# The first two tiles of a four-layer residual chain interleaved: the second tile's narrow chunk moved ahead of the first tile's later chunks

## The chip, the core and the metric

One core of a Trainium2 chip runs the whole program. The metric is the device time of one execution in microseconds (us). TensorE (PE) multiplies matrices, VectorE (DVE), ScalarE (ACT) and GpSimd (POOL) work on elements, SyncE (SP) issues most of the transfers. PEld is PE's loading of stationary operands, beside its matmuls. Each engine works through its own list in order, and semaphores tie the lists together.

## The reference

`x` has 64 batches of 32 rows of 512. Four layers follow each other, each added to its input. The start of the program, which the change touches, is all in the first of them:

```python
def lora_add(base, inp, A, B):
    Ab = A[layer_idx][lora_indices]
    Bb = B[layer_idx][lora_indices]
    t = jnp.einsum('bri,bni->bnr', Ab, inp)
    return base + jnp.einsum('bor,bnr->bno', Bb, t) * SCALE
gate = lora_add(jnp.einsum('bnh,fh->bnf', x, W_gate), x, A_gate, B_gate)
up = lora_add(jnp.einsum('bnh,fh->bnf', x, W_up), x, A_up, B_up)
act = jax.nn.silu(gate) * up
down = lora_add(jnp.einsum('bnf,hf->bnh', act, W_down), act, A_down, B_down)
...
x = x + _L0_cond_ref(...)
x = x + _L1_cond_ref(x, itok_B_0_15, L1_cond_weights)
x = x + _L2_cond_ref(...)
x = x + _L3_cond_ref(x, L3_cond_weights, itok_B_0_15)
```

F is 1376, the rank is 16, and each batch picks its own adapter (A and B) by an index. Layers 1 and 3 multiply each batch by a small matrix of its own, layer 2 is a projection with a routed adapter.

## The kernel before

The 2048 rows are cut into 16 tiles of 128 rows (four batches each). The first layer runs over all tiles, then the other three do. F is cut into three chunks: chunk 0 is the narrow one with 352 columns, chunks 1 and 2 have 512. A step is one chunk of one tile; before the change step s is chunk `s % 3` of tile `s // 3`. I write (tile, chunk), so (1,0) is the narrow chunk of the second tile.

Every float32 operand of a matmul is split in two parts, a high one that ACT writes (a cast, `hi`) and a low one that DVE writes (raw minus high, `lo`); for the weights `wd` of the down product POOL writes the low part instead. `product` is then three matmuls (lines 1050 to 1052), `stacked` two (1057 and 1058). The weights are loaded and split once, in the beginning, and stay.

For one tile PE does: `gate` and `up` of a chunk (12 matmuls each, over four pieces of 128 of the 512 inputs); `x_a`, x times the chosen adapters A, which from the second tile on is part of the narrow chunk's gate matmuls (480 columns instead of 352 and 128); `transpose_t`, after DVE has masked that result (`tm`, line 846); `adapters` (four matmuls, the B part, which ends the chunk); `transpose_act`, after ACT's silu (`gate` job, line 691) and DVE's product with up (line 885); `down` (18 matmuls for chunk 0, 24 for the others, adding up in `down_ps`); and once for a tile `transpose_td` and `down_adapters`, after DVE's mask `td`. The gate and up of a step stand in one of two pairs of PSUM banks.

The adapters come by indirect transfers that POOL issues: `a` (four gathers for a tile, one for each batch) and `b` (one for each chunk), `bd` one for each tile. `a_raw` holds one tile, so the next tile's gathers wait until both of its splits are done: `at`, for `x_a`, and `adt`, for the down side. `b_sel` has two slots: the gather of step s waits until the adapters of step s - 2 have run.

The order of the splits and of the silus is written by hand in `lane_jobs(s)`, one list for ACT and DVE both, and `gathers(s)` with the `wd` pieces of that list gives POOL's order. `plain_loads(s)` orders SP's loads.

Of the kernel before, what the change touches and what calls it, by code (L numbers as in the profile page):

```python
# [68 lines left out]
W13_FIRST = 6  # L69
# [58 lines left out]

def plain_loads(s):

    i, n = divmod(s, NC)
    if s < 0:
        first = wgu_items(0, 0)
        return ([("x", 0, 0), first[0], first[1], ("x", 0, 1)] + first[2:] + wgu_items(0, 1)
                + wgu_items(1, 0) + [("wd", f) for f in pieces_of(0)] + wgu_items(1, 1)
                + wgu_items(2, 0) + [("wd", f) for f in pieces_of(1)] + wgu_items(2, 1)
                + [("x", 1, 0)] + [("wd", f) for f in pieces_of(2)])
    return [("x", i + 1, 0)] if n == 0 and 1 <= i < NT - 1 else []


def gathers(s):
# [59 lines left out]
NO_SPLIT = ("gate", "tm", "x1")  # L201


def bass_conditioned_residual_chain(nc, x_t, x_rows, it_lora, it_cond, it_lang, wgu, wd, a_all, b_d,
# [7 lines left out]
    with ExitStack() as ctx:  # L212
# [1118 lines left out]
```

## Time and profile before

| | us |
|---|---|
| median of three runs (610.81 to 610.93) | 610.91 |
| the profiled execution | 610.14 |
| its span | 608.3 |
| PE busy in the span | 574.6 |
| DVE, ACT, POOL busy | 324.8, 204.8, 232.2 |

The profiled execution is 0.77 us shorter than the median, and its time is its span and 1.84 us around it. PE is busy in 94% of the span. The span's slices of a fortieth are 15.2 us each: the first 60 us, nearly four of them, hold 20.5 of the 33.7 us in which PE isn't busy (39.54 us of them are busy).

### The profile page before, as it was taken

How to read it: one execution, taken by the hardware profiler on the slowest of the kernel's cores; microseconds unless marked ns; L12 is line 12 of the kernel's file. 1: busy time of each engine (PE TensorE's matmuls, PEld its weight loads, DVE VectorE, ACT ScalarE, POOL GpSimd, SP SyncE). 2: the span in 40 equal slices, each digit the busy share in tenths (PEclk: the TensorE clock that was granted, in tenths of full speed). 3: DMA queues.
4: the chain of work that ended last, by engine and by line, in shares of the span. 5: the costliest groups of instructions: out<-in, count | busy, mean ns of one | idle time of the engine just before them, and what ended most of it. 6: DMA issues, size and time to landing. Idle time of an engine off the chain costs nothing.

```text
span 608.3 us, 8713 instructions
## 1 busy us (share of the span) xinstructions
PE 574.6 (94%) x3359; PEld 515.5 (85%) x3359; DVE 324.8 (53%) x686; ACT 204.8 (34%) x413; POOL 232.2 (38%) x238
## 2 busy tenths in 40 slices
PE   4578999999999999999999999999999998999896
PEld 3467898989898988898988989898989888988894
DVE  3596434344344444343534344434444668899986
ACT  3654233233233232332323332332332433343331
POOL 4276425243443434332313131323322435556631
PEclk9689999999999999999999999999999999999999
DMA  8951524242434242433333242423334310322211
GB/s 271 367 180 52 170 75 135 75 136 80 130 110 122 99 141 88 129 101 114 109 94 130 75 131 73 132 73 130 97 108 152 126 53 19 99 76 70 71 70 70
DMA packets 30281, 68.99 MB, mean 113 GB/s; under 512 B 4704, under 2 KB 9120, under 8 KB 30240
## 3 DMA queue, kind: packets, MB, share of 16 engines
q0 software_dynamic: 10752, 37.23, 19.5%
q1 hardware_dynamic: 19344, 31.17, 15.5%
q8 instruction: 27, 0.44, 0.3%
q14 instruction: 14, 0.11, 0.1%
q10 hardware_dynamic: 144, 0.03, 0.0%
HBM read 60.03 MB, written 8.39 MB: 112 GB/s over the span
## 4 chain that ended last, share of the span: by engine, by line
PE 80%; DVE 11%; DMA 2%; issue 2%; ACT 2%; POOL 1%; SPq 1%; POOLq 0%; DVEq 0%; ACTq 0%
PE gu_ps L1050 13%; PE gu_ps L1052 13%; PE gu_ps L1051 13%; PE down_ps L1050 7%; PE down_ps L1051 7%; PE down_ps L1052 7%; PE gu_ps L1057 3%; PE gu_ps L1058 3%; PE act_t L1116 3%; PE l_ps L1050 2%; PE l_ps L1052 2%; PE l_ps L1051 2%; DVE route L949 2%; DVE x L967 2%; DVE route L948 1%
## 5 line engine op out<-in xcount | busy, mean ns | idle before, releaser
L576 POOL DMA_INDIRECT b_sel_raw<-b_gu,idx_rank x48 | 45.7, 952 | 225.4 <-PE gu_ps L1058 222.3
L1050 PE MATMUL gu_ps<-w_sb,xt 128*128 128x512 f32 x256 | 105.8, 413 | 4.4 <-DVE w_sb L837 4.4
L1050 PE MATMUL down_ps<-wd_sb,act_hl 128*128 128x288 f32 (+1 forms) x352 | 105.1, 298 | 0.2 <-DVE act_hl L837 0.2
L1051 PE MATMUL down_ps<-wd_sb,act_hl 128*128 128x288 f32 (+1 forms) x352 | 103.8, 295 | 0.0
L1052 PE MATMUL down_ps<-wd_sb,act_hl 128*128 128x288 f32 (+1 forms) x352 | 103.7, 295 | 0.0
L1052 PE MATMUL gu_ps<-w_sb,xt 128*128 128x512 f32 x256 | 101.8, 397 | 0.0
L1051 PE MATMUL gu_ps<-w_sb,xt 128*128 128x512 f32 x256 | 101.4, 396 | 0.0
L576 POOL DMA_INDIRECT a_raw<-a_all,idx_batch x64 | 76.1, 1190 | 48.1 <-DVE wd_sb L837 28.7
L698 ACT CAST act_hl<-act_t 128x256 fp32r<-128x256 f32 (+1 forms) x64 | 27.3, 452 | 149.6 <-PE act_t L1116 149.6
L691 ACT ACTIVATE act<-gu_ps 128x512 f32<-128x512 f32 (+1 forms) x48 | 26.5, 553 | 132.7 <-PE gu_ps L1058 132.6
L837 DVE TENSOR_TENSOR act_hl<-act_t,act_hl 128x256 fp32r<-128x256 f32 (+1 forms) x64 | 32.0, 520 | 70.3 <-ACT act_hl L698 70.3
L885 DVE TENSOR_TENSOR act<-act,gu_ps 128x512 f32<-128x512 f32 (+1 forms) x48 | 30.3, 632 | 73.1 <-ACT act L691 73.1
L1050 PEld LDWEIGHTS down_ps<-wd_sb,act_hl 128*128 128x128 f32 (+1 forms) x352 | 66.1, 188 | 1.7 <-DVE act_hl L837 0.4
L1051 PEld LDWEIGHTS down_ps<-wd_sb,act_hl 128*128 128x128 f32 (+1 forms) x352 | 66.2, 188 | 1.2
L1052 PEld LDWEIGHTS down_ps<-wd_sb,act_hl 128*128 128x128 f32 (+1 forms) x352 | 66.1, 188 | 0.0
L837 DVE TENSOR_TENSOR b_sel<-b_sel_raw,b_sel 128x1024 fp32r<-128x1024 f32 (+1 forms) x48 | 53.8, 1121 | 15.3 <-ACT b_sel L675 15.3
L1050 PEld LDWEIGHTS gu_ps<-w_sb,xt 128*128 128x128 f32 x256 | 48.8, 191 | 13.4 <-issue 3.1
L1052 PEld LDWEIGHTS gu_ps<-w_sb,xt 128*128 128x128 f32 x256 | 48.8, 190 | 11.1
L1051 PEld LDWEIGHTS gu_ps<-w_sb,xt 128*128 128x128 f32 x256 | 49.1, 192 | 7.2
L675 ACT CAST b_sel<-b_sel_raw 128x1024 fp32r<-128x1024 f32 (+1 forms) x48 | 45.6, 950 | 3.3 <-DMA b_sel_raw<-b_gu,idx_rank 3.3
L1050 PE MATMUL l_ps<-w2ra_hl,x2t_hl 128*128 128x328 f32 (+1 forms) x128 | 42.8, 334 | 1.3 <-DVE x_res L876 1.0
L1051 PE MATMUL l_ps<-w2ra_hl,x2t_hl 128*128 128x328 f32 (+1 forms) x128 | 39.8, 311 | 0.0
(126 smaller groups left out, 1121.4 us busy)
## 6 DMA issues: line engine op xcount, KB each, us to landing
w_sb_raw<-wgu SPq DMA_DIRECT2D x16, 256.0 KB, 8.1
x_res<-x_rows SPq DMA_DIRECT2D x16, 256.0 KB, 3.3
x_after_l<-x_res SPq DMA_DIRECT2D x16, 256.0 KB, 2.1
x<-x_after_l SPq DMA_DIRECT2D x16, 256.0 KB, 2.7
xt_raw<-x_t SPq DMA_DIRECT2D x15, 256.0 KB, 2.5
out<-y SPq DMA_DIRECT2D x15, 256.0 KB, 2.0
wd_sb_raw<-wd SPq DMA_DIRECT2D x10, 256.0 KB, 8.7
w2ra_hl_raw<-w2ra_t SPq DMA_DIRECT2D x4, 324.0 KB, 4.8
```

The source lines that it names most:

```text
L576: nc.gpsimd.indirect_dma_start(out=dst, out_offset=None, in_=table, in_offset=bass.IndirectOffsetOnAxis(ap=idx, axis=0)).then_inc(s, 16)
L675: sc.copy(out_, in_).then_inc(s_hi, 1)
L691: sc.activation(act[:, s % 2, 0:width(s % NC)], gate_of(s), ACT.Silu).then_inc(s_silu, 1)
L698: ins = sc.copy(act_hl[0:k, s % 2, 0, j0:j1, :], act_t[0:k, j0:j1, :])
L837: return ve.tensor_tensor(out_, raw, high.bitcast(F32), ALU.subtract)
L885: ve.tensor_tensor(a, a, up_of(s), ALU.mult).then_inc(s_mul, 1)
L1050: pe.matmul(out_, stationary[0], moving[0], start=start, stop=False, skip_group_check=True)
L1051: pe.matmul(out_, stationary[0], moving[1], start=False, stop=False, skip_group_check=True)
L1052: return pe.matmul(out_, stationary[1], moving[0], start=False, stop=stop, skip_group_check=True)
L1057: pe.matmul(out_, stationary, moving[0], start=False, stop=False, skip_group_check=True)
L1058: return pe.matmul(out_, stationary, moving[1], start=False, stop=True, skip_group_check=True)
L1116: mm = pe.transpose(act_t[0:w, j, :], act[:, s % 2, j * P:j * P + w], ident)
```

## The change

The first six steps get another order, `ORDER`: (0,0), (0,1), (1,0), (0,2), (1,1), (1,2). From the third tile on the steps are as before. What PE does from the start to the adapters of (2,0) is written out call by call, and there (0,0) is followed at once by gate and up of (1,0), ahead of `x_a(0)`. Steps are numbered by their place in `ORDER`, so `gate(2)` is the gate of (1,0) and `adapters(4)` those of (1,1); `down(d)` and `transpose_act(d)` count as before, tile by tile, so `down(2)` is that of (0,2). Gate and up of (1,0) stand in the banks of `down_ps`, which are not in use yet, and its act in the second half of `x_res`. For the second tile `x_a` is a call of its own too. `t_hl` gets two slots.

The lists of ACT, DVE, POOL and SP for these steps are written out as well. The load and the split of the second tile's x go up ahead of everything of chunks 1 and 2, the computation of the indices for the `b` gathers goes up on DVE into the split of the first weights, and POOL has a list of its own, `pool_jobs`. The indices of the later layers are computed two steps later (`s == 4`), and their gathers start two steps later (`W13_FIRST`).

```diff
-W13_FIRST = 6
+W13_FIRST = 8
...
+ORDER = [(0, 0), (0, 1), (1, 0), (0, 2), (1, 1), (1, 2)] + [(i, n) for i in range(2, NT) for n in range(NC)]
+FREE = 6
...
+def slot(s):
+    return (0, 1, 2, 0, 1, 0)[s] if s < FREE else (s + 1) % 2
...
+def first_items():
+    w = wgu_items(0, 0)
+    return [("x", 0, 0), w[0], w[1], ("x", 0, 1), w[2], w[3]] + wgu_items(0, 1) + [("x", 1, 0)]
...
 def plain_loads(s):
-    i, n = divmod(s, NC)
     if s < 0:
-        first = wgu_items(0, 0)
-        return ([("x", 0, 0), first[0], first[1], ("x", 0, 1)] + first[2:] + wgu_items(0, 1)
-                + wgu_items(1, 0) + [("wd", f) for f in pieces_of(0)] + wgu_items(1, 1)
-                + wgu_items(2, 0) + [("wd", f) for f in pieces_of(1)] + wgu_items(2, 1)
-                + [("x", 1, 0)] + [("wd", f) for f in pieces_of(2)])
-    return [("x", i + 1, 0)] if n == 0 and 1 <= i < NT - 1 else []
-
-
-def gathers(s):
-
-    i, n = divmod(s, NC)
-    if s < 0:
-        return [("a", 0, b) for b in range(TB)] + [("b", 0), ("b", 1)]
+        return (first_items() + wgu_items(1, 0) + wgu_items(1, 1) + wgu_items(2, 0) + wd_items(0) + wgu_items(2, 1)
+                + wd_items(1) + wd_items(2))
+    if s == 4:
+        return [("x", 2, 0)]
+    i, n = ORDER[s]
+    return [("x", i + 1, 0)] if n == 0 and 2 <= i < NT - 1 else []
...
+def pool_jobs(s):
+    if s < FREE:
+        return {-1: a_items(0) + [("b", 0), ("b", 1)],
+                0: a_items(1) + [("b", 2)],
+                1: [("b", 3)] + wd_items(0) + [("bd", 0)],
+                2: wd_items(1) + [("b", 4)] + a_items(2),
+                3: [("b", 5)] + wd_items(2),
+                4: [("b", 6)],
+                5: [("bd", 1)]}[s]
...
+    if s <= FREE:
+        w2u = wgu_items(2, 1)
+        return {-1: first_items() + [("at", 0)],
+                0: wgu_items(1, 0) + [("tm", 0), ("b", 0), ("t", 0), ("adt", 0)] + wgu_items(1, 1)
+                + [("b", 1), ("gate", 0)],
+                1: wgu_items(2, 0) + wd_items(0) + [("gate", 1), ("at", 1), ("act", 0), w2u[0], w2u[1], ("tm", 1),
+                                                    w2u[2], w2u[3]],
+                2: [("b", 2), ("t", 1), ("b", 3), ("gate", 2), ("adt", 1)],
+                3: [("gate", 3)] + wd_items(1) + [("act", 1), ("b", 4)],
+                4: [("gate", 4), ("bd", 0), ("act", 2)] + wd_items(2) + [("b", 5), ("x", 2, 0)],
+                5: [("tdm", 0), ("td", 0), ("act", 3), ("x1", 0), ("at", 2), ("gate", 5), ("b", 6)],
+                6: [("act", 4), ("tm", 2), ("act", 5), ("t", 2), ("adt", 2), ("bd", 1), ("tdm", 1), ("gate", 6),
+                    ("b", 7)]}[s]
-    if s < 0:
-        first = wgu_items(0, 0)
-        return [("x", 0, 0), first[0], first[1], ("x", 0, 1)] + first[2:] + wgu_items(0, 1) + [("at", 0), ("b", 0)]
-    if s == 0:
-        return ([("tm", 0), ("t", 0)] + wgu_items(1, 0) + [("gate", 0)] + [("wd", f) for f in pieces_of(0)]
-                + [("adt", 0)] + wgu_items(1, 1) + [("b", 1)])
-    if s == 1:
-        return ([("act", 0)] + wgu_items(2, 0) + [("wd", f) for f in pieces_of(1)] + [("gate", 1)] + wgu_items(2, 1)
-                + [("b", 2)])
-    if s == 2:
-        return ([("act", 1), ("x", 1, 0), ("at", 1), ("gate", 2)] + [("wd", f) for f in pieces_of(2)]
-                + [("b", 3), ("adt", 1)])
...
+        t_hl = sb("t_hl", [2, 2, P], F32R, mem_a)
...
+        def bank(s, m):
+            return gu_ps[slot(s)][m][:] if slot(s) < 2 else down_ps[:, m, :]
...
+        def act_of(s):
+            w = width(ORDER[s][1])
+            return act[:, slot(s), 0:w] if slot(s) < 2 else x_res[:, 1, 0:w]
...
+                for job in pool_jobs(s):
...
-                    if job == ("at", 0):
+                    if job == ("wgu", 0, 0, 2):
...
-                if s == 2:
+                if s == 4:
...
-            for s in range(STEPS):
-                i, n = divmod(s, NC)
+            def whole(part, s):
+                part(s, 0, HC)
+
+            whole(gate, 0)
+            whole(up, 0)
+            whole(gate, 2)
+            whole(up, 2)
+            x_a(0)
+            gate(1, 0, HC // 2)
+            transpose_t(0)
+            gate(1, HC // 2, HC)
+            adapters(0)
+            whole(up, 1)
+            adapters(1)
+            whole(gate, 3)
+            x_a(1)
+            transpose_act(0)
+            up(3, 0, HC // 2)
+            transpose_t(1)
+            up(3, HC // 2, HC)
+            adapters(2)
+            adapters(3)
+            down(0)
+            whole(gate, 4)
+            transpose_act(1)
+            whole(up, 4)
+            adapters(4)
+            down(1)
+            transpose_act(2)
+            gate(5, 0, HC // 2)
+            down(2)
+            gate(5, HC // 2, HC)
+            transpose_td(0)
+            transpose_act(3)
+            up(5, 0, HC // 2)
+            down_adapters(0)
+            up(5, HC // 2, HC)
+            adapters(5)
+            down(3)
+            transpose_act(4)
+            whole(gate, 6)
+            down(4)
+            transpose_act(5)
+            whole(up, 6)
+            transpose_t(2)
+            down(5)
+            adapters(6)
+            for s in range(FREE + 1, STEPS):
```

On POOL, the stretch from the second tile's `a` gathers on. `a_raw` are the `a` gathers, `b_sel_raw` the `b` gathers (`b_gu1` is chunk 1's table), TENSOR_TENSOR the low parts of `wd`. Before:

```order
L576 DMA a_raw<-a_all,idx_batch 128x304 x2
L576 DMA b_sel_raw<-b_gu2,idx_rank 128x1024
L645 TENSOR_TENSOR wd_sb<-wd_sb_raw,wd_sb 128x2x256 x4
L576 DMA a_raw<-a_all,idx_batch 128x304 x2
L576 DMA b_sel_raw<-b_gu0,idx_rank 128x704
L645 TENSOR_TENSOR wd_sb<-wd_sb_raw,wd_sb 128x2x256 x4
L576 DMA bd_hl_raw<-b_d,idx_rank 128x512
L576 DMA b_sel_raw<-b_gu1,idx_rank 128x1024
```

And with the change, from the same gathers on:

```order
L642 DMA a_raw<-a_all,idx_batch 128x304 x4
L642 DMA b_sel_raw<-b_gu0,idx_rank 128x704
L642 DMA b_sel_raw<-b_gu2,idx_rank 128x1024
L708 ISA
L708 TENSOR_TENSOR wd_sb<-wd_sb_raw,wd_sb 128x2x256 x2
L708 TENSOR_TENSOR wd_sb<-wd_sb_raw,wd_sb 96x2x256
L642 DMA bd_hl_raw<-b_d,idx_rank 128x512
L708 TENSOR_TENSOR wd_sb<-wd_sb_raw,wd_sb 128x2x256 x4
L642 DMA b_sel_raw<-b_gu1,idx_rank 128x1024
L642 DMA a_raw<-a_all,idx_batch 128x304 x4
```

All low parts of `wd` now come after the second tile's `a` gathers, and the second table-1 gather, which is that of (1,1), stands right behind the four low parts of chunk 1's `wd`.

On ACT, the place of the `wd` casts (each line here is the high part of what its name says, ACTIVATE is the silu). Before:

```order
L675 CAST w2_sb<-w2_sb_raw 128x512 x4
L675 CAST wd_sb<-wd_sb_raw 128x2x256 x4
L691 ACTIVATE act<-gu_ps1_0 128x512
L675 CAST w2_sb<-w2_sb_raw 128x512 x4
L675 CAST b_sel<-b_sel_raw 128x1024
L698 CAST act_hl<-act_t 128x512
```

And with the change:

```order
L738 CAST b_sel<-b_sel_raw 128x1024
L754 ACTIVATE x_res<-down_ps 128x352
L742 CAST wd_sb<-a_raw 128x11x32 x2
L754 ACTIVATE act<-gu_ps0_0 128x512
L738 CAST wd_sb<-wd_sb_raw 128x2x256 x4
L761 CAST act_hl<-act_t 128x512
L738 CAST b_sel<-b_sel_raw 128x1024
L754 ACTIVATE act<-gu_ps1_0 128x512
L738 CAST bd_hl<-bd_hl_raw 128x512
L761 CAST act_hl<-act_t 128x512
L738 CAST wd_sb<-wd_sb_raw 128x2x256 x4
```

The casts of chunk 1's `wd` stood ahead of the silu of (0,1); now they stand behind the silu of (0,2), and those of chunk 2 behind the high part of (0,2)'s transposed act.

On DVE, what stands around the second tile's `at` (the low part `wg0_sb<-a_raw`, which `x_a(1)` needs). Before:

```order
L837 TENSOR_TENSOR act_hl<-act_t,act_hl 128x512
L837 TENSOR_TENSOR xt1<-xt1_raw,xt1 128x512
L837 TENSOR_TENSOR wg0_sb<-a_raw,wg0_sb 128x4x128
L885 TENSOR_TENSOR act<-act,gu_ps0_1 128x512
L837 TENSOR_TENSOR b_sel<-b_sel_raw,b_sel 128x704
```

And with the change:

```order
L900 TENSOR_TENSOR w2_sb<-w2_sb_raw,w2_sb 128x512 x4
L948 TENSOR_TENSOR act<-act,gu_ps1_1 128x512
L900 TENSOR_TENSOR wg0_sb<-a_raw,wg0_sb 128x4x128
L900 TENSOR_TENSOR act_hl<-act_t,act_hl 128x256
L900 TENSOR_TENSOR act_hl<-act_t,act_hl 96x128
L900 TENSOR_TENSOR w2_sb<-w2_sb_raw,w2_sb 128x512 x2
```

It moved from behind all weights of gate and up to ahead of the last four of them, chunk 2's up weights.

## Rows read from the trace of the kernel before

**Rows 1.** The profile's page: PE's share; the clock granted in 40 equal slices.
```profile
PE 574.6 (94%) x3359; PEld 515.5 (85%) x3359; DVE 324.8 (53%) x686; ACT 204.8 (34%) x413; POOL 232.2 (38%) x238
PEclk9689999999999999999999999999999999999999
```

**Rows 2.** PE's waits, first 130 us: what for, us in total, times, longest.
```profile
PE gu_ps L1050 <- DVE wg_sb L837: 10.9, 2, 6.5
PE gu_ps L1050 <- DVE w_sb L837: 4.4, 2, 2.9
PE t_ps L1096 <- DVE t_m L846: 4.0, 2, 2.6
PE gu_ps L1057 <- DVE t_hl L837: 1.0, 1, 1.0
```

**Rows 3.** PE's timeline: start, duration, operation, [idle before and releaser].
```profile
17.14 0.33 PE L1050 MATMUL gu_ps<-wg_sb,xt 128*128 128x128 f32 x1 [4.37 <-DVE wg_sb L837]
...
17.75 0.27 PE L1052 MATMUL gu_ps<-wg_sb,xt 128*128 128x128 f32 x1
...
40.60 0.47 PE L1050 MATMUL gu_ps<-w_sb,xt 128*128 128x512 f32 x1 [2.91 <-DVE w_sb L837]
...
42.12 0.63 PE L1050 MATMUL gu_ps<-w_sb,xt 128*128 128x512 f32 x1
...
44.68 0.94 PE L1116 MATMUL act_t<-const_sb,act 128*128 128x128 f32 x4
45.38 0.48 PE L1050 MATMUL gu_ps<-w_sb,xt 128*128 128x512 f32 x1
...
49.10 0.29 PE L1050 MATMUL down_ps<-wd_sb,act_hl 128*128 128x288 f32 x1
...
52.26 0.38 PE L1050 MATMUL gu_ps<-wg_sb,xt 128*128 128x480 f32 x1
...
55.21 0.41 PE L1050 MATMUL gu_ps<-wu_sb,xt 128*128 128x352 f32 x1
...
92.13 0.40 PE L1050 MATMUL gu_ps<-w_sb,xt 128*128 128x512 f32 x1
```

**Rows 4.** ACT's timeline, four places.
```profile
15.68 0.62 ACT L679 CAST wg_sb<-a_raw 128x512 fp32r<-128x512 f32 x1 [5.05 <-DMA a_raw<-a_all,idx_batch]
...
49.30 0.60 ACT L691 ACTIVATE act<-gu_ps 128x512 f32<-128x512 f32 x1 [2.02 <-PE gu_ps L1058]
49.80 2.17 ACT L675 CAST wd_sb<-wd_sb_raw 128x512 fp32r<-128x512 f32 x4
...
63.82 1.04 ACT L675 CAST b_sel<-b_sel_raw 128x1024 fp32r<-128x1024 f32 x1
```

**Rows 5.** DVE's timeline, four places.
```profile
23.39 2.50 DVE L837 TENSOR_TENSOR w_sb<-w_sb_raw,w_sb 128x512 fp32r<-128x512 f32 x4
...
27.81 1.16 DVE L837 TENSOR_TENSOR wd_sb<-a_raw,wd_sb 128x352 fp32r<-128x352 f32 x1 [1.37 <-ACT wd_sb L679]
...
34.54 5.92 DVE L837 TENSOR_TENSOR w_sb<-w_sb_raw,w_sb 128x512 fp32r<-128x512 f32 x1
...
64.89 1.23 DVE L837 TENSOR_TENSOR b_sel<-b_sel_raw,b_sel 128x1024 fp32r<-128x1024 f32 x1 [0.41 <-ACT b_sel L675]
```

**Rows 6.** POOL's timeline, three places.
```profile
9.37 0.95 POOL L576 DMA_INDIRECT a_raw<-a_all,idx_batch  x1 [0.30 <-issue]
...
27.30 1.28 POOL L645 TENSOR_TENSOR wd_sb<-wd_sb_raw,wd_sb 128x512 fp32r<-128x512 f32 x1
...
34.91 4.99 POOL L645 TENSOR_TENSOR wd_sb<-wd_sb_raw,wd_sb 128x512 fp32r<-128x512 f32 x4
```

**Rows 7.** Gathers, issue to landing: `a` at 5 to 10 us, at 30.5 to 33 us, `b` at 40 to 100 us.
```profile
DMA to landing us min/median/max: 5.5/6.2/6.8
...
DMA to landing us min/median/max: 3.6/3.9/4.2
...
DMA to landing us min/median/max: 3.4/3.9/4.5
```

More of the change, by code:

```diff
@@ L118, with step_of, slot_before, down_no @@
 CONSTS = const_array()
+ORDER = [(0, 0), (0, 1), (1, 0), (0, 2), (1, 1), (1, 2)] + [(i, n) for i in range(2, NT) for n in range(NC)]
+FREE = 6
+def step_of(i, n):
+    return ORDER.index((i, n))
+def slot(s):
+    return (0, 1, 2, 0, 1, 0)[s] if s < FREE else (s + 1) % 2
+def slot_before(s):
+    return max((k for k in range(s) if slot(k) == slot(s)), default=None)
+def down_no(s):
+    i, n = ORDER[s]
+    return i * NC + n
+def gu_done(i):
+    return step_of(i, NC - 1) + 1
 def x_pieces(i):
@@ L272, in bass_conditioned_residual_chain @@
         banks_a = ExitStack()
-        gu_ps = [[ps(f"gu_ps{i}_{m}", [H], banks_a) for m in range(2)] for i in range(2)]
+        gu_ps = {i: [ps(f"gu_ps{i}_{m}", [H], banks_a) for m in range(2)] for i in (1, 0)}
         down_ps = ps("down_ps", [2, H], banks_a)
@@ L637, in _ @@
             for s in range(-1, STEPS):
-                first = [it for it in gathers(s) if s < 0 or it[0] == "b"]
-                for it in first:
-                    gather_item(it)
-                for job in lane_jobs(s):
+                for job in pool_jobs(s):
                     if job[0] == "wd":
@@ L645, in _ @@
                         pool.tensor_tensor(l, raw, h.bitcast(F32), ALU.subtract).then_inc(s_wdlo, 1)
-                for it in gathers(s)[len(first):]:
-                    gather_item(it)
+                    else:
+                        gather_item(job)
                 if s == STEPS - 2:
@@ L879, in job_lo @@
                     s = job[1]
-                    i, n = divmod(s, NC)
-                    if n == 0 and i >= 1:
-                        mask_td(i - 1)
                     ve.wait_ge(s_silu, s + 1)
-                    a = act[:, s % 2, 0:width(n)]
+                    a = act_of(s)
                     ve.tensor_tensor(a, a, up_of(s), ALU.mult).then_inc(s_mul, 1)
@@ L895, in job_lo @@
                 elif kind == "t":
-                    ins = lo(t_hl[TR:, :, :], t_ps[TR:, 0:2, :], t_hl[TR:, :, :])
+                    own = t_hl[TR:, job[1] % 2, :, :]
+                    ins = lo(own, t_ps[TR:, 0:2, :], own)
                 elif kind == "td":
@@ L1130, in down @@
                         pe.wait_ge(s_wdlo, WD_ORDER.index(f) + 1)
-                    a_hl = [act_hl[0:w, s % 2, part, j, :] for part in range(2)]
+                    a_hl = [act_hl[0:w, d % 2, part, j, :] for part in range(2)]
                     for half in range(2):
@@ L1232, in _ @@
                 if n == 0:
-                    if i == 0:
-                        x_a(0)
                     transpose_t(i)
@@ L1239, in _ @@
                     transpose_x2(0)
-                if s >= 1:
-                    down(s - 1)
+                down(s - 1)
                 if n == 0:
```

142 lines of the change are left out of this document (81 added, 61 removed).

## The prediction, as put on record before the changed kernel had run

> **What bounds the kernel now.** The page comes first: PE is busy in 94% of the span, and the clock row falls below 9 in two slices only, the second (6) and the third (8) [rows 1]. So the kernel is bound by PE's own work, and what is left to gain in the beginning is holes and slow clock. The waits of PE name the holes: 10.9 us for `wg_sb` (6.5 of them the first load, the rest the 4.37 us ahead of `x_a(0)`), 4.4 us for weights, 4.0 for the mask of t and 1.0 for its low part [rows 2]. The timeline of PE then gives the price of each piece of work at the full clock: from 45.38 to 49.10 us there are 16 matmuls of 512 columns, 0.2325 us each, so a gate or up of 512 columns takes 2.79 us and its adapters 0.93; by columns a gate of 352 takes 1.92 and its adapters 0.64. Down takes 3.16 us for four pieces (49.10 to 52.26) and 2.37 for three. From 52.26 to 55.21 stand a gate of 480 columns (2.62) and the transposes of act, which leaves 0.33 for these. `x_a` takes 12 times 0.61 / 5, 1.46 us [rows 3].
>
> With these prices all of PE's work up to the first matmul of (2,1), at 92.13 us, comes to 63.4 us: four blocks of 352 columns (7.7) and eight of 512 (22.3) for the two tiles, adapters 5.0, downs 17.4, transposes and the down adapters 3.6, one `x_a` 1.5, the 128 extra columns of the second tile's gate 0.7, and 5.2 for (2,0). PE starts at 6.5 [rows 2], so 22.2 us are lost by then: 13.8 in the holes of [rows 2], the other 8.4 to half clock and restarts. After 92.13 nothing in the program changes its order in a way that I expect to matter: the later gathers and indices are moved by two steps where PE doesn't wait, and `t_hl` gets a second slot where nobody waited for one. So I forecast the time of that one matmul, and the difference is that of the kernel.
>
> **The change, part by part.** *Gate and up of (1,0) ahead of `x_a(0)`.* PE ended up(0,0) at 12.8 us and idled 4.37 [rows 3]. The three small index operations now ahead of the third weight's split cost it about 0.25. Then 2 x 1.92 us of new work lie in the hole, to 16.8. `x_a(0)` still starts at 17.14, since the gathers of `a` land at 15.68 as before and their cast and low part take 1.46 to the first matmul [rows 3, 4]. All but 0.3 us of the hole is filled.
>
> *Up to the gate of (0,2).* DVE needs 2.50 us for four weights [rows 5], from 17.1 to 19.6, then the mask of t, so the transposes of t come at 20.1 (a hole of 0.2) and adapters(0) end at 22.45. `adt(0)` stands ahead of chunk 1's up weights and ends at 22.75; the first of these is ready at 23.4, a hole of 0.9. Up(0,1) ends at 26.2, adapters(1) at 27.25, gate(0,2) at 30.2. PE has then done 19.4 us of work in 23.7, and 3.8 of that is (1,0)'s.
>
> *`x_a(1)`.* Its gathers wait for `adt(0)`. With 0.95 + 0.30 us each [rows 6] the last of the four is issued at 26.8. At 30 us, under as full a DMA, such gathers landed 3.6 to 4.2 us after issue, and at 5 to 10 us 5.5 to 6.8 [rows 7]; the later stretch is the nearer one, since SP's backlog is the same, and 3.9 gives 30.7, and 1.46 more 32.2. PE, done with gate(0,2) at 30.2, idles. DVE's low part, at 31.4, meets POOL: its two `b` gathers end at 30.3 and then come three low parts of `wd`, about 1.25 us each. The rows show two outcomes of such a meeting. At 27.81 DVE came into a running POOL operation (27.30 to 28.58) and ended 0.4 after it. At 34.54 it took 5.92 us for 0.65 us of work, until POOL had done all four, at 39.90 [rows 5, 6]. I take the first, 32.4 us; the second gives 34.6. The Trainium skill's page "SBUF — State Buffer", section "Who interferes with whom", says that a DVE operation with two SBUF inputs and a GpSimd operation that reads SBUF exclude each other, the later one waiting for the whole of the earlier. By that rule the wait would be to the end of one operation, as at 27.81; the row at 34.54 is worse than the rule.
>
> *From there to the end of adapters(3), which I call T.* `x_a(1)` and the transposes of act end at 34.2. The cast, the low part and the first of chunk 2's up weights (0.55 + 0.63 + 0.63, from rows 4 and 5, and the hand-overs) let up(0,2) start at 36.2, a second hole of 2.0. DVE then has in a row four weights (2.5), a mask (0.5), the low parts of b(1,0), t and b(0,2) (0.9, 0.4, 1.15), from 35.5 to 40.9; adapters(3) follow. T is 42.0. By then PE has done 25.9 us of a total that is now 64.1 (`x_a(1)` apart costs 0.7 more), and 38.2 are left. Without a further hole the mark would stand at 80.2, 11.9 ahead of 92.13.
>
> *adapters(4), of (1,1).* This is where I expect the lead to go. The `b` gather of (1,1) stands on POOL behind the four low parts of chunk 1's `wd`, their casts on ACT behind the silu of (0,2), and this behind adapters(3). After T: silu 0.2 later and 0.5 long before the next [rows 3, 4], first cast 0.7, so POOL starts at T + 1.4; 4.99 for four [rows 6]; gather issued at T + 6.5; landing 3.9 (3.4 to 4.5) [rows 7]; cast and low part of b 2.3 (63.82 to 66.12) [rows 4, 5]. That is T + 12.8. PE has down(0), gate and up of (1,1) and transposes until then, 2.37 + 2.79 + 0.33 + 2.79 = 8.3. The hole is 4.5 us, 4.0 to 5.1 by the bounds of the landing.
>
> *The clock.* After the 4.37 us hole and after the 2.91 us hole the granted clock fell to 1.2 GHz: from 42.12 to 44.68 six matmuls took 0.427 each, and it was back by 45.38 [rows 3]. A hole of 4.5 us should do the same. Each microsecond at the low clock loses 0.46; with 3.3 us of it 1.5 are lost, and the second slice's 6 shows that it can last longer [rows 1]. I take 2.0, with 0 and 2.7 as bounds. The two holes around `x_a(1)`, 2.2 and 2.0 with 1.8 of work between, are each shorter than 2.91, and I take no clock loss there.
>
> *down(2), of (0,2).* Its `wd` casts stand behind the cast of its own act. From the start of its transposes, POOL starts 1.8 later, and a piece is ready every 1.25, where PE needs one each 0.79. PE would end 4.9 after the transposes began and ends 7.6 after; the low parts of b(1,2) and of the third tile's x on DVE meet the same POOL operations and cost one more, 1.1, and the mask of td behind them some 0.3. I take 4.1, with 2.7 and 5.0 as bounds.
>
> The sum: 42.0 + 38.2 + 4.5 + 2.0 + 4.1, and 0.3 for restarts, is 91.1, against 92.13: 1.0 us less. The profiled execution took 610.14, so 609.1 there, and 609.9 against the median, which is 0.77 above that execution.
>
> **The rivals.** *The later holes are cheaper* (0.22). The clock stays up after the hole and b lands in 3.4 instead of 3.9: 2.0 + 0.5 less, 607.4. For it speaks that at 40.60 PE resumed at the full clock and only by 42.12 had lost it, so that a fall isn't certain [rows 3]; against it, that both holes of this length were followed by one.
>
> *POOL holds DVE off at `x_a(1)`* (0.24), the one that ends slower. DVE waits for all three low parts of `wd`: `x_a(1)` at 34.6 instead of 32.4. The hole is then 4.4 us, as long as the one ahead of 17.14, and the half clock falls on up(0,2), another 1.6: 613.7. It decides for slower from a start of `x_a(1)` at about 34.5, or 33.5 with the clock down. For it speaks the row at 34.54; gathers that land in 6.2 us would end in the same place.
>
> *The change does what its order seems made for* (0.06): the gathers and `wd` parts are ready in time, and the lead of 11.9 stays: 599. The chain behind T is four POOL operations and a gather in one queue, so I see little for it.
>
> **How the numbers follow.** The forecast's own case has 0.46, with 608.4 to 611.4 as its range. About 0.2%, 1.2 us, is what a measurement of this kernel can tell from no change. Of the 0.46, 0.15 lie over 1.2 us faster, 0.26 within and 0.05 slower; the cheaper holes, the full gain and 0.01 of the rest are faster, POOL's hold and 0.01 of the rest slower. That makes 0.44, 0.26 and 0.30. The range of 606.3 to 614.0 leaves out the full gain, the bottom of the cheaper case and the top of the slower one.
>
> **What would show it.** Right: PE has no hole over 1 us between 6.54 and 30; one of about 2 ahead of `x_a(1)`; one over 4 ahead of adapters(4), ended by the low part of b, whose gather follows four low parts of `wd` on POOL; matmuls of down(2) in groups of six every 1.25 us with POOL as what they wait for; the first matmul of (2,1) at 91. Wrong: a `b` gather of (1,1) that lands before PE has done up(1,1); a hole at the transposes of t or at up(0,1) much above 1 us, because ACT has more to cast early than I counted; or a change after the 92 us mark.

## The result, and the profile after

The changed kernel takes 615.56 us (median of 4 runs, 614.74 to 616.72), the kernel before 610.86 on the same chip (4 runs, 610.47 to 610.93). The ratio is 1.008, with a 95% interval of 1.0062 to 1.0097: 0.8% slower. The prediction was 609.9, with 606.3 to 614.0 as its range, so the direction and the range are both missed. The profiled execution after took 616.72, its span is 614.9.

The page of the changed kernel, with its engines and its clock row, answers to [rows 1]:

```profile
PE 579.2 (94%) x3371; PEld 518.2 (84%) x3371; DVE 317.3 (52%) x686; ACT 204.8 (33%) x413; POOL 231.7 (38%) x238
...
PEclk9969899999999999999999999999999999999999
```

PE's share is still 94%, though it is busy for 4.6 us more than before; part of that is the low clock. The 6 and the 8 of the clock row, in the second and third slice before, are now in the third and the fifth (a slice is 15.4 us). The waits of PE in the first 120 us of the changed kernel (sum, times, longest), for [rows 2]:

```profile
PE gu_ps L1114 <- DVE wg_sb L900: 6.8, 2, 6.6
PE down_ps L1114 <- DVE wg_sb L900: 5.4, 1, 5.4
PE gu_ps L1121 <- DVE b_sel L900: 4.7, 2, 4.5
PE down_ps L1114 <- POOL wd_sb L708: 3.1, 3, 1.3
PE gu_ps L1114 <- DVE w_sb L900: 2.7, 2, 1.9
```

The hole ahead of `x_a(0)` is gone (6.8 holds only the first load and 0.3). A hole of 5.4 stands ahead of `x_a(1)` (`down_ps` is where the second tile's `x_a` writes), and one of 4.5 for a `b_sel`. The timeline of PE gives their places, where [rows 3] had theirs; the number ahead of the arrow in brackets is the idle time, and the row at 48.07 is the start of down(0), behind adapters(3):

```profile
16.96 0.33 PE L1114 MATMUL gu_ps<-wg_sb,xt 128*128 128x128 f32 x1 [0.27 <-DVE wg_sb L900]
23.03 0.50 PE L1114 MATMUL gu_ps<-w_sb,xt 128*128 128x512 f32 x1 [0.79 <-DVE w_sb L900]
35.65 0.48 PE L1114 MATMUL down_ps<-wg_sb,xt 128*128 128x128 f32 x1 [5.41 <-DVE wg_sb L900]
41.01 0.80 PE L1114 MATMUL gu_ps<-w_sb,xt 128*128 128x512 f32 x1 [1.87 <-DVE w_sb L900]
48.07 0.29 PE L1114 MATMUL down_ps<-wd_sb,act_hl 128*128 128x288 f32 x1
61.03 0.80 PE L1121 MATMUL gu_ps<-b_sel,t_hl 128*128 128x512 f32 x1 [4.46 <-DVE b_sel L900]
70.50 0.37 PE L1114 MATMUL down_ps<-wd_sb,act_hl 128*128 128x288 f32 x1 [1.26 <-POOL wd_sb L708]
73.95 0.40 PE L1114 MATMUL down_ps<-wd_sb,act_hl 128*128 128x288 f32 x1 [1.22 <-POOL wd_sb L708]
75.63 0.48 PE L1114 MATMUL down_ps<-wd_sb,act_hl 128*128 128x288 f32 x1 [0.62 <-POOL wd_sb L708]
```

Up to 30.24, the end of gate(0,2), PE follows the forecast to within 0.4 us: `x_a(0)` at 16.96 after 0.27, up(0,1) at 23.03 after 0.79. Then it waits until 35.65. What it waits for is seen on three other engines of the changed kernel, POOL (the last of the four gathers, the low parts of chunk 0's and of chunk 1's `wd`, and the `b` gather of (1,1) behind these), ACT and DVE, for [rows 4 to 6]:

```profile
27.08 1.45 POOL L642 DMA_INDIRECT a_raw<-a_all,idx_batch  x1 [0.30 <-issue]
...
31.14 3.71 POOL L708 TENSOR_TENSOR wd_sb<-wd_sb_raw,wd_sb 128x512 fp32r<-128x512 f32 x3
...
49.45 5.04 POOL L708 TENSOR_TENSOR wd_sb<-wd_sb_raw,wd_sb 128x512 fp32r<-128x512 f32 x4 [13.02 <-ACT wd_sb L738]
...
54.63 0.96 POOL L642 DMA_INDIRECT b_sel_raw<-b_gu,idx_rank  x1
```

```profile
34.25 0.62 ACT L742 CAST wg_sb<-a_raw 128x512 fp32r<-128x512 f32 x1 [5.36 <-DMA a_raw<-a_all,idx_batch]
...
58.67 1.04 ACT L738 CAST b_sel<-b_sel_raw 128x1024 fp32r<-128x1024 f32 x1 [4.23 <-DMA b_sel_raw<-b_gu,idx_rank]
...
99.34 0.47 ACT L754 ACTIVATE act<-gu_ps 128x352 f32<-128x352 f32 x1 [2.18 <-PE gu_ps L1122]
```

```profile
34.90 0.69 DVE L900 TENSOR_TENSOR wg_sb<-a_raw,wg_sb 128x512 fp32r<-128x512 f32 x1 [5.29 <-ACT wg_sb L742]
```

The last gather is issued at 27.08, and ACT, idle for 5.36 us, gets its data at 34.25: 7.2 us, where I had 3.9 [rows 7]. DVE's low part then takes 0.69. POOL had ended its three operations at 34.85, 0.05 ahead of it. The hole ahead of adapters(4) is as forecast: the `b` gather follows the four low parts at 54.63, and its data is there at 58.67, 4.0 later. What PE lost besides the holes is in windows of PE alone (window and its length, PE busy and its instructions, granted clock as a share of 2.4 GHz; the last two columns are the DMA engines' share and GB/s):

```profile
30.00:35.00 5.00, 0.24 (x2) 0.98 1.08 361
35.00:45.00 10.00, 7.48 (x25) 0.50 0.28 100
45.00:58.00 13.00, 11.31 (x59) 1.00 0.24 80
58.00:66.00 8.00, 4.97 (x19) 0.57 0.49 148
66.00:75.50 9.50, 6.38 (x39) 1.00 0.00 0
75.50:80.00 4.50, 4.37 (x17) 0.62 0.26 80
80.00:100.00 20.00, 20.00 (x129) 1.00 0.25 82
```

Three stretches run at 1.2 GHz: all of 35 to 45, most of 58 to 66, and 3.4 us after 75.5. The silu of (2,0), which waits for the end of its gate and starts 0.20 after the mark of the prediction in the kernel before (92.33), starts at 99.34: 7.0 later. Behind it nothing has changed: time less mark is 610.14 - 92.33 = 517.8 us before and 616.72 - 99.34 = 517.4 after. I use this silu as the mark below.

### The profile page after: what moved, and what is told of

Its sections match the earlier page's. It is cut to its first block, busy times and chain, and to the rows that moved or that the text cites. A ratio compares the mean times of both kernels' runs of the same rounds, so it can differ in the third digit from the quotient of the medians.

```text
span 614.9 us, 8736 instructions
## 1 busy us (share of the span) xinstructions
PE 579.2 (94%) x3371; PEld 518.2 (84%) x3371; DVE 317.3 (52%) x686; ACT 204.8 (33%) x413; POOL 231.7 (38%) x238
## 3 DMA queue, kind: packets, MB, share of 16 engines
q1 hardware_dynamic: 19344, 31.17, 15.4%
## 4 chain that ended last, share of the span: by engine, by line
PE 79%; DVE 9%; POOL 4%; DMA 3%; ACT 2%; issue 2%; POOLq 0%; DVEq 0%; ACTq 0%
PE gu_ps L1114 12%; PE gu_ps L1116 12%; PE gu_ps L1115 12%; PE down_ps L1114 8%; PE down_ps L1115 7%; PE down_ps L1116 7%; PE gu_ps L1121 3%; PE gu_ps L1122 3%; PE act_t L1184 3%; PE l_ps L1114 2%; PE l_ps L1116 2%; PE l_ps L1115 2%; DMA a_raw<-a_all,idx_batch 2%; DVE route L1013 2%; POOL wd_sb L708 2%
## 5 line engine op out<-in xcount | busy, mean ns | idle before, releaser
L1114 PEld LDWEIGHTS down_ps<-wd_sb,act_hl 128*128 128x128 f32 (+1 forms) x352 | 66.8, 190 | 5.7 <-POOL wd_sb L708 2.7
L1115 PEld LDWEIGHTS down_ps<-wd_sb,act_hl 128*128 128x128 f32 (+1 forms) x352 | 67.0, 190 | 1.3
L1116 PEld LDWEIGHTS down_ps<-wd_sb,act_hl 128*128 128x128 f32 (+1 forms) x352 | 66.9, 190 | 0.0
L1114 PE MATMUL l_ps<-w2ra_hl,x2t_hl 128*128 128x328 f32 (+1 forms) x128 | 42.8, 334 | 1.3 <-DVE x_res L942 1.0
L1121 PE MATMUL gu_ps<-b_sel,t_hl 128*128 128x512 f32 (+1 forms) x94 | 35.5, 378 | 4.7 <-DVE b_sel L900 4.7
## 6 DMA issues: line engine op xcount, KB each, us to landing
wd_sb_raw<-wd SPq DMA_DIRECT2D x10, 256.0 KB, 11.9
```

The lines of the kernel that those rows point to most:

```text
L1114: pe.matmul(out_, stationary[0], moving[0], start=start, stop=False, skip_group_check=True)
L1115: pe.matmul(out_, stationary[0], moving[1], start=False, stop=False, skip_group_check=True)
L1116: return pe.matmul(out_, stationary[1], moving[0], start=False, stop=stop, skip_group_check=True)
L1121: pe.matmul(out_, stationary, moving[0], start=False, stop=False, skip_group_check=True)
```

## The experiments

Each ran beside the kernel before and names times of its own; ratios are to the kernel before, so the changed kernel stands at 1.008. The medians of the kernel before were 610.0 to 610.2 beside the experiments and 610.86 beside the changed kernel, so a gain told as a difference to 615.56 may be 0.7 to 0.9 us too large. Marks are from the profiled execution alone; time less mark lies between 516.0 and 517.5 in all of them. Lines in rows shift by two or four where an edit adds code.

**Theory A**: the four gathers share the DMA engines with SP's backlog of weights, so they land late; PE, idle for 5.4 us, comes back at half clock. **Theory B**: POOL's low parts keep DVE off (the rival of the prediction), and an earlier landing would change nothing. (The Theory B in the expectation of experiment 4 is another one, gathers that are slow in themselves.) For the hole ahead of adapters(4): the order on POOL.

**1. The `b` gather ahead of the four low parts.**

```diff
-                2: wd_items(1) + [("b", 4)] + a_items(2),
+                2: [("b", 4)] + wd_items(1) + a_items(2),
```

> The changed kernel with one edit: POOL issues the b gather of (1,1) ahead of the four low parts of chunk 1's wd instead of behind them. Theory 1 (the hole ahead of adapters(4) is POOL's queue, and the half clock after it is its follower): the 4.46 us hole shrinks below 0.5, the clock stays up from 58.8 to 65.7 us, which is worth another 2.1, and the time falls by 6.5 to about 609. Theory 2 (the clock falls anyway, from the holes before and after): only the hole goes, about 611. Theory 3 (the gather is slow in itself or ACT has no time for its cast): the hole stays over 3 us, 615.

Measured: 607.36 us (606.71 to 609.17), ratio 0.9955 [0.9936, 0.9975], mark 92.92, below all three forecasts. The gather is issued at 48.61 instead of 54.63 and the hole of 4.46 is gone. Two stretches of half clock go with it, as the windows of PE in this kernel show:

```profile
30.00:48.00 18.00, 10.74 (x36) 0.62 0.50 165
48.00:60.00 12.00, 11.65 (x63) 1.00 0.33 108
60.00:72.00 12.00, 8.79 (x56) 1.00 0.22 78
```

Exchanging one gather with four low parts is worth 8.2 us by the medians and 7.6 by the ratios, and turns the change from 0.8% slower into 0.45% faster. Waits of down(2) are still 3.1 us here, all inside 60 to 72, and the clock stays at 1.00: those waits alone don't lower it.

**2. The `wd` casts of chunk 2 early.**

```diff
-                3: [("gate", 3)] + wd_items(1) + [("act", 1), ("b", 4)],
-                4: [("gate", 4), ("bd", 0), ("act", 2)] + wd_items(2) + [("b", 5), ("x", 2, 0)],
+                3: [("gate", 3)] + wd_items(1) + wd_items(2) + [("act", 1), ("b", 4)],
+                4: [("gate", 4), ("bd", 0), ("act", 2)] + [("b", 5), ("x", 2, 0)],
```

> The changed kernel with one edit: ACT casts chunk 2's wd right behind chunk 1's, three steps of its list earlier, so that POOL can do the low parts ahead of down(2). Theory 1: the three waits of down(2) for POOL (3.1 us) go, the mask of td is no longer late, and the half clock from 75.9 to 79.3 (1.6 us) doesn't come: 4 to 5 us less, about 611. Rival: the half clock isn't tied to these waits, 3 us less, 612.5. Second rival: the earlier low parts collide with DVE's low part of bd and PE waits there instead, 615.

Measured: 610.78 (610.13 to 611.45), ratio 1.001 [0.9995, 1.0025], mark 93.58, as the first theory had it. The waits of down(2) are gone, and so is the half clock after 75.5; the hole ahead of adapters(4) is 4.3, with its half clock. The term of down(2) was in the prediction and is real. In experiment 1 the waits stay and the second stretch of half clock goes, here the second stretch stays and the waits go, and in neither does the third stretch come. The two aren't enough for it either: experiment 4 has both and no third stretch (granted clock 1.00 from 70 to 80).

**3. `adt(0)` right behind `at(0)`**, so that `a_raw` comes free and the second tile's gathers start 4.5 us earlier.

```diff
-        return {-1: first_items() + [("at", 0)],
-                0: wgu_items(1, 0) + [("tm", 0), ("b", 0), ("t", 0), ("adt", 0)] + wgu_items(1, 1)
+        return {-1: first_items() + [("at", 0), ("adt", 0)],
+                0: wgu_items(1, 0) + [("tm", 0), ("b", 0), ("t", 0)] + wgu_items(1, 1)
```

> The changed kernel with one edit: adt(0), both splits of the first tile's down-side adapters, right behind at(0), so that the second tile's a gathers can be issued at about 18 us instead of 22.6. Theory 1 (x_a(1) waits for gathers that land about 7 us after issue): they land by about 30, the hole of 5.41 us ahead of x_a(1) falls under 1, the half clock from 34.9 to 45.2 (3.4 us) doesn't come, a new hole of 0.7 opens at gate(0,1): 7 to 8 us less, about 608. Rival (the DMA is the limit, and the gathers land at 34 whatever their issue): 615.5 or a little more.

Measured: 614.05 (613.75 to 615.05), ratio 1.0076 [1.005, 1.0102], mark 97.71. A miss, and the most useful run. The gathers were issued from 18.04 to 22.54, landed 6.2 to 6.9 us after their issue, beside the same full queue of weights, and were no longer waited for. But POOL's list moved up too, and its low parts met DVE at the weights of gate(0,2). The timeline of POOL, the group of the four splits of these weights on DVE (duration in ns: least, median, most), and the timeline of PE in this kernel:

```profile
28.47 3.73 POOL L708 TENSOR_TENSOR wd_sb<-wd_sb_raw,wd_sb 128x512 fp32r<-128x512 f32 x3
```

```profile
L900 DVE TENSOR_TENSOR w_sb<-w_sb_raw,w_sb x4: 684/686/4677, 26.3 to 28.1; 128x512 fp32r<-128x512 f32 x4
```

```profile
32.81 0.50 PE L1114 MATMUL gu_ps<-w_sb,xt 128*128 128x512 f32 x1 [3.40 <-DVE w_sb L900]
```

Three splits take 0.69 us and the fourth 4.68: it started at 28.08, 0.39 ahead of POOL's first, and ended at 32.76, 0.56 behind the end of the last of POOL's three operations (32.20). The hole that was ahead of `x_a(1)` now stands inside gate(0,2), ahead of its last weight, 3.4 us long and again followed by half clock.

**4. SP holds back the up weights of chunk 2 until the gathers have landed.** This tells A from B: it takes the load off the DMA engines and leaves POOL's list as it is. It also makes the held loads themselves later.

```diff
+                    if it == ("wgu", 2, 1, 0):
+                        sp.wait_ge(s_a_in, 16 * TB * 2)
```

> The changed kernel with one edit: SP holds the loads of chunk 2's up weights and all behind it until the second tile's a gathers have landed. Theory A (the gathers land late because the weight loads share the DMA with them): the last one lands 4 us after its issue instead of 7.2, x_a(1) starts at 32.5 instead of 35.65, but chunk 2's up weights come later, so that the second hole grows: 611 to 614. Theory B (four gathers in a row are slow by themselves, about 75 GB/s): the landing stays at 34, and the held loads cost time: 617 or more.

Measured: 615.17 (614.77 to 616.27), ratio 1.0094 [1.0067, 1.0121]. The time is in neither forecast, and both causes named above, A and B, are real, one behind the other. That four gathers are slow in themselves is refuted: they land early here. ACT, POOL and DVE in this kernel:

```profile
31.32 0.62 ACT L744 CAST wg_sb<-a_raw 128x512 fp32r<-128x512 f32 x1 [2.36 <-DMA a_raw<-a_all,idx_batch]
```

```profile
27.14 1.45 POOL L644 DMA_INDIRECT a_raw<-a_all,idx_batch  x1 [0.30 <-issue]
...
31.19 3.71 POOL L710 TENSOR_TENSOR wd_sb<-wd_sb_raw,wd_sb 128x512 fp32r<-128x512 f32 x3
```

```profile
31.97 3.49 DVE L902 TENSOR_TENSOR wg_sb<-a_raw,wg_sb 128x512 fp32r<-128x512 f32 x1 [2.29 <-ACT wg_sb L744]
```

The gather lands 4.2 us after its issue instead of 7.2 (A). From 20 to 36 us SP's queue took 82.8% of the DMA engines' time in the changed kernel and takes 41.4% in this one (queue: packets, MB, share of 16 engines):

```profile
q1 hardware_dynamic: 3644, 4.27, 82.8%
```

```profile
q1 hardware_dynamic: 1571, 2.22, 41.4%
```

DVE's low part, ready 2.9 us earlier, starts into POOL's first operation (31.19) and takes 3.49 us instead of 0.69, until 0.56 after the third one's end. `x_a(1)` starts at 35.52 after a hole of 5.19, where it was 35.65 and 5.41 (B). Each cause hides the other: with the gathers in time, PE is only 0.13 us earlier.

**5. The same, with POOL waiting for that low part** before its first `wd` low part.

```diff
+                        if job == ("wd", pieces_of(0)[0]):
+                            pool.wait_ge(s_lo, s_lo_of(("at", 1)))
```

> The changed kernel with SP's held loads (alone 615.2), and POOL's first low part of wd waits until DVE has done the low part of at(1). Theory 1 (in the run with held loads the gathers landed at 31.3 and DVE's low part then took 3.49 us instead of 0.69, because POOL's three low parts of wd kept it out): DVE's operation takes 0.7, x_a(1) starts at 32.8 instead of 35.5, 2.7 us less, and up to 3 more if the half clock after the hole stays away: 609 to 612.5. Rival (DVE was slow for another reason): 615.

Measured: 612.03 (610.45 to 613.13), ratio 1.0032 [1.0016, 1.0047], mark 96.51. DVE takes 0.69 us at 31.73, and `x_a(1)` starts at 32.47 after a hole of 2.40: the very time (32.4) and hole (2.2) that the prediction had. Since the weights were held back (ACT waits 1.84 us for their load at 36.79), the next hole grew from 1.87 to 3.81, so this is no fair price of the forecast's case; it shows the place, not the sum.

**6. Experiment 3 with POOL waiting.**

> The changed kernel with adt(0) right behind at(0) (alone 614.0), and POOL's first low part of wd waits until DVE has done the low part of at(1). Theory 1 (alone, the gathers were in time, but POOL's low parts kept DVE from the last weight of gate(0,2) for 4.68 us): no hole over 1 us up to x_a(1), which starts near 30.5, no half clock from 33 to 43: 606 to 608. Rival (the low parts of wd, now later, keep DVE from chunk 2's up weights instead): 611 to 614.

Measured: 609.28 (605.97 to 613.75), ratio 0.9981 [0.9956, 1.0005], mark 92.61, between the two forecasts. The holes are 0.38 ahead of `x_a(1)` at 30.54, 2.44 behind it and 4.42 ahead of adapters(4). Against the changed kernel that is 6.3 us for the hole of 5.41 and most of the half clock behind it (the low stretch is 3.4 us instead of 10.2). A half clock does come, from 35.0 on, behind the hole of 2.44. The runs spread over 7.8 us, more than with any other kernel here.

**7. Experiments 1 and 2 together.**

> The changed kernel with both single edits, the b gather of (1,1) ahead of chunk 1's low parts (alone 607.4) and chunk 2's wd cast behind chunk 1's (alone 610.8), against 615.6 without. Theory 1 (each removes a hole and the half clock that follows it, and they don't share these): the gains of 8.2 and 4.8 add up to 602.6. Rival (the second one's gain is mostly a half clock that the first one already keeps away): 605 to 606.

Measured: 607.11 (604.53 to 607.25), ratio 0.9934 [0.9908, 0.9959], mark 89.64. Apart they gained 8.2 and 4.8 us against the changed kernel by the medians, together 8.5; by the mark 6.4 and 5.8, together 9.7. That is worse than the rival's 605 to 606. They share the third stretch of half clock. In this kernel the clock is 1.00 from 48 on and 0.62 in 30 to 48, as in experiment 1. By either count the gains don't add up, but how much the second edit adds to the first isn't settled by them: 0.3 us by the medians, 1.3 by the ratios, 3.3 by the mark.

**8. All of it**: 1, 2 and 3, the first two up weights of chunk 2 ahead of `at(1)`, and POOL waiting.

```diff
-                1: wgu_items(2, 0) + wd_items(0) + [("gate", 1), ("at", 1), ("act", 0), w2u[0], w2u[1], ("tm", 1),
+                1: wgu_items(2, 0) + wd_items(0) + [("gate", 1), w2u[0], w2u[1], ("at", 1), ("act", 0), ("tm", 1),
```

> The changed kernel with all edits: b gather of (1,1) first, chunk 2's wd cast early, adt(0) early, the first two of chunk 2's up weights ahead of at(1), and POOL held until at(1)'s low part is done. Theory 1 (the lead of about 12 us that gate and up of (1,0) bring is real and was given back in holes, port waits and half clock): 594 to 598. Rival (ACT and DVE have no room, and holes open elsewhere): 600 or more.

Measured: 598.69 (597.16 to 599.77), ratio 0.9805 [0.9781, 0.9829], mark 82.98. That is between the two forecasts. PE's longest waits from 12 to 100 us in this kernel, and two windows of PE:

```profile
PE down_ps L1116 <- DVE wg_sb L902: 1.7, 1, 1.7
PE t_ps L1212 <- DVE td L922: 0.8, 1, 0.8
PE t_ps L1164 <- DVE t_m L911: 0.6, 1, 0.6
PE down_ps L1116 <- POOL wd_sb L710: 0.4, 2, 0.2
```

```profile
12.00:50.00 38.00, 34.87 (x173) 0.96 0.82 281
50.00:83.00 33.00, 31.68 (x198) 1.00 0.29 93
```

Of the lead of 11.9 us that the prediction worked out for the first 42 us (599 as a rival's time), 9.35 are left at the mark, and the time is 11.5 below that of the kernel before by the medians: the interleaving keeps most of its lead, if the lists of POOL, DVE and ACT are ordered for it. What the same care with the lists would give without the interleaving isn't shown; experiment 10 tries only one wait there.

**9. The same without POOL's wait**, which prices the meeting of POOL and DVE by itself.

> The combined kernel of 598.7 without the one wait that holds POOL's low parts of wd until the low part of at(1). Theory (consecutive low parts on POOL keep a waiting DVE operation out until the last of them is done): one DVE operation near 28 to 29 us takes 4 us or more instead of 0.65, x_a(1) starts at about 35.5 instead of 32.1, and the half clock follows: 602 to 604. Rival (DVE gets in between two POOL operations, as the one at 27.81 did before): 599 to 600.

Measured: 603.00 (602.67 to 604.13), ratio 0.9887 [0.9863, 0.9911], mark 86.64. DVE and PE in this kernel:

```profile
26.31 6.50 DVE L900 TENSOR_TENSOR w_sb<-w_sb_raw,w_sb 128x512 fp32r<-128x512 f32 x4
```

```profile
32.87 0.50 PE L1114 MATMUL gu_ps<-w_sb,xt 128*128 128x512 f32 x1 [3.40 <-DVE w_sb L900]
```

Four splits that take 2.49 us in experiment 8 take 6.50 here: three of them 0.69, as there, and the last 4.70, from 28.11 to 32.81. POOL, in this kernel, began its three low parts 0.41 behind it and ended them at 32.25:

```profile
28.52 3.73 POOL L708 TENSOR_TENSOR wd_sb<-wd_sb_raw,wd_sb 128x512 fp32r<-128x512 f32 x3
```

`x_a(1)` starts at 35.27, as forecast. One wait of POOL, for which nobody waits, is worth 4.3 us.

**10. The same medicine for the kernel before**: there POOL's low parts of chunk 1 wait for the last gate weight of chunk 2 (the meeting at 34.54 in [rows 5, 6]).

```diff
+                        if job == ("wd", pieces_of(1)[0]):
+                            pool.wait_ge(s_lo, s_lo_of(("wgu", 2, 0, HC - 1)))
```

> The kernel before, with one edit: POOL's low parts of chunk 1's wd wait until DVE has done the low part of the last of chunk 2's gate weights. Theory (the DVE operation of 5.92 us at 34.54 was kept out by four POOL operations, and that made the hole of 2.91 us and the half clock after it): it takes 0.7, gate(0,2) starts at 37.5 instead of 40.6, and if chunk 2's up weights don't meet POOL in turn, the time falls by 3 to 4.5, to 606 to 607. Rival (they do meet, and up(0,2) waits instead): within 1 of before.

Measured: 611.20 (610.34 to 612.33), ratio 1.0015 [0.9999, 1.003], mark 94.46. The gate weights are split in 2.48 us now, but POOL starts on its four at 37.46 and the up weights meet it instead:

```profile
37.46 6.39 POOL L647 TENSOR_TENSOR wd_sb<-wd_sb_raw,wd_sb 128x512 fp32r<-128x512 f32 x4 [2.20 <-DVE w_sb L839]
```

```profile
37.90 6.50 DVE L839 TENSOR_TENSOR w_sb<-w_sb_raw,w_sb 128x512 fp32r<-128x512 f32 x4
```

This is the milder meeting: the engines take turns, DVE's four splits with 1.4 to 1.8 us each and POOL's four operations with 1.3 to 1.8. Behind POOL's late operations stand the gathers of the second tile, and a hole of 3.26 us comes at 58.35, where the kernel before has one of 1.39 at 58.76; that the one makes the other wasn't tested. So the gain of experiment 8 isn't to be had by this wait alone.

**11 and 12. PE's own order around the last hole** (1.75 us ahead of `x_a(1)` in experiment 8). In the first, half of up(0,2) goes ahead of `x_a(1)`:

```diff
             whole(gate, 3)
+            up(3, 0, HC // 2)
             x_a(1)
             transpose_act(0)
-            up(3, 0, HC // 2)
             transpose_t(1)
```

> The combined kernel of 598.7 with PE's first half of up(0,2) ahead of x_a(1) instead of behind the transposes of act. Theory: the hole of 1.75 us ahead of x_a(1) is filled, a hole of about 1.8 comes ahead of the transposes of t instead, whose mask is now the last to be ready, and adapters(2) start 0.9 earlier: 597 to 598. If the half clock (3.4 us in the profile before) goes too, 596.

Measured: 599.42 (598.19 to 600.09), ratio 0.9817 [0.9795, 0.9838], mark 82.67. A miss: the hole moved to the transposes of t at 35.58 (1.67 us, for the mask), with 3.4 us of half clock behind it, and nothing was gained. In the second the other half goes ahead of the transposes too, and all up weights of chunk 2 are split before act(0), POOL waiting for the last of them:

```diff
-            up(3, 0, HC // 2)
-            transpose_t(1)
             up(3, HC // 2, HC)
+            transpose_t(1)
```

> As the run before, and all of chunk 2's up weights ahead of the first act on ACT and DVE, up(0,2) in full ahead of the transposes of t, POOL held until the last of these weights is done. Theory: PE has no hole up to the transposes of t, but the low part of b(1,0) meets POOL's low parts of wd and is kept out until 37: adapters(2) start 1 us earlier than at 598.7: 596 to 598. If b's low part gets in at once, 595.

Measured: 598.41 (597.41 to 599.36), ratio 0.9804 [0.9783, 0.9826], mark 82.22. The one hole is now several, none over 1.03 us from 12 us on, and this is the only kernel whose clock never fell in the first 100 us: its clock row has a 9 in every slice.

```profile
PEclk9999999999999999999999999999999999999999
```

It can't be told from experiment 8, though the low part of b(1,0) did get in at once, for which the expectation had 595. DVE's row for it, and POOL's low parts around it:

```profile
36.16 0.90 DVE L902 TENSOR_TENSOR b_sel<-b_sel_raw,b_sel 128x704 fp32r<-128x704 f32 x1
```

```profile
33.79 4.40 POOL L710 TENSOR_TENSOR wd_sb<-wd_sb_raw,wd_sb 128x512 fp32r<-128x512 f32 x3 [4.48 <-DVE w_sb L902]
```

Experiments 8 and 12 are about 2% faster than the kernel before and by their medians 2.7 to 2.8% faster than the changed kernel.

## Why the prediction was wrong

The mark was forecast at 91.1, 91.3 for the silu, and came at 99.34: 8.0 us late.

**The hole ahead of `x_a(1)`, +3.3.** The first step that failed: "the later stretch is the nearer one, since SP's backlog is the same, and 3.9 gives 30.7". SP's backlog wasn't the same: it was issuing eight loads of `wd` from 19.79 to 27.99, beside the four gathers, where the kernel before issued the last four from 23.33 to 26.45, and its pair came 4.3 us after these. The last of the four gathers landed in 7.2 us, beyond both groups of [rows 7] (the higher one, 5.5 to 6.8, would have been nearer). Experiment 4 shows the cause: with SP's loads held back it is 4.2. But it also shows that the right landing would not have saved the forecast, since DVE's low part then takes 3.49 us and `x_a(1)` starts at 35.52. So the 3.3 are the price of two steps, either of which is enough: this one and "I take the first, 32.4 us", below. The rows at 30.5 to 33 us were those of a pair of gathers, and what the change has there is the last of a set of four, with its issue stretched as well (1.45 us instead of 0.95).

**The clock, up to +4.5.** "I take no clock loss there" failed: I had the hole at 2.2 because of the step above, and it was 5.4. PE then ran at 0.50 through all of 35 to 45, where it was busy for 7.48 us. With half of the time lost at the low clock (the prediction's 0.46), the three windows give 3.4, some 2.2 for the 4.7 us that it was busy from 61.03 to 65.7, and 1.5 for the 3.3 us after 75.5: 7.1 in all, against a term of 2.0. Not all of the 3.4 arrives: from `x_a(1)` to the end of adapters(3) it took 12.4 us (35.65 to 48.07) instead of 9.6 (32.4 to 42.0), 2.8 more, since the forecast had PE wait for DVE there anyway. Behind it the clock cost 3.7 instead of 2.0. Two of the three stretches I hadn't foreseen; the one that I had, behind the hole ahead of adapters(4), cost what I said.

**The hole ahead of adapters(4)** was right: 4.5 forecast, 4.46 measured, by the low part of b behind the four low parts on POOL, as experiment 1 shows by moving it. **down(2)** was right in kind, 3.1 against 4.1, a gain of 1.0. **The start** was right to 0.4 us until 30.2. These terms and the clock's make 3.3 + 2.8 + 1.7 - 1.0 = 6.8 of the 8.0. The other 1.2 us lie behind adapters(3), which ended 6.1 us late, and aren't placed.

**The rivals.** That POOL holds DVE off at `x_a(1)` was given 0.24 and 613.7. The hold is real (experiments 3, 4, 9), but in the changed kernel it didn't happen: the gathers were so late that POOL had just finished. The outcome that this rival described, `x_a(1)` at 34.5 or later and half clock on up(0,2), came by way of the other sentence in it, on gathers that land in over 6.2 us. Of the two outcomes of a meeting that the trace of before showed, I took the mild one. This is the second step that failed, "I take the first, 32.4 us", though the changed kernel alone doesn't show it: the meetings on PE's path in experiments 3, 4 and 9 went the other way, with 4.68, 3.49 and 4.70 us for one operation. Experiment 5, which takes both away, has `x_a(1)` at 32.47. The Trainium skill's page "SBUF — State Buffer", section "Who interferes with whom", lets the later of the two wait for the whole of the earlier instruction; the measurements decide against that as an upper bound: the operations of 3.49, 4.68 and 4.70 us ended 0.56 behind the third of POOL's operations of 1.24 each, and not behind the first, and those of experiments 3 and 9 were by their recorded starts the earlier of the two. That the full lead is kept was given 0.06, and this change didn't keep it; experiments 8 and 12 show that most of the lead was there.

**The total.** Behind the mark nothing moved (517.8 and 517.4), as forecast.

## What to carry to other kernels

Moving a consumer up moves its producers into other traffic: take the landing time of a transfer from a stretch with the same number of other transfers outstanding, and where none is alike, take the worst row, knowing that it may be too low (6.8 here, against 7.2). When two late things arrive together, removing one shows little (experiments 3 and 4); look at what each engine did at that moment, and remove both. An engine with slack can still be the cheapest one to hold back: a wait on POOL that nobody is waiting behind gave 4.3 us, but in the kernel before, where POOL then met the next weights, it gave nothing.

## What the runs showed of the hardware

- A DVE operation with two inputs in SBUF that runs beside such operations back to back on POOL may last until all of them are done: 3.49, 4.68 and 4.70 us instead of 0.69 beside three (experiments 4, 3, 9), 5.92 beside four (34.54 in [rows 5]). The one of 3.49 started 0.78 us behind the start of POOL's first operation, the others 0.37 to 0.41 ahead of it. It isn't always so: the row at 27.81 ended 0.4 after one of POOL's, in experiment 10 the engines took turns, and in experiment 12 an operation in the middle of POOL's three took 0.90, as without them. What decides is open.
- POOL pays too: the four low parts that took 5.04 us in the changed kernel at 49.45 took 6.39 in experiment 10, where they took turns with DVE.
- The last of four gathers landed 7.2 us after its issue beside a full queue of weight loads, and 4.2 with that queue held back. In experiment 3 the four took 6.2 to 6.9.
- PE's low clock after a hole lasted for very different times: 10.2 us after the 5.41 and 1.87 of the changed kernel, 13.7 after the same two holes (5.39 and 1.87) in experiment 1, and 3.4 after one of 1.75 in experiment 8 and one of 1.67 in experiment 11. In experiment 12, with no hole over 1.03 us, the clock didn't fall. What sets these lengths wasn't tested.
